# The last stage of an attention and mixture-of-experts kernel: half of each returned row block is added by accumulating transfers

## The chip, the cores and the metric

The kernel runs on one core of one Trainium2 chip. The metric is the device time of one execution in microseconds; lower is better. The time of the kernel before is 515.96 us, the median of three runs (512.97 to 517.47).

## The reference

The input is 64 sequences of 64 tokens, 4096 tokens of 256 numbers. First comes an attention layer over the tokens and a context, then a feed-forward layer of 32 experts, of which each token uses four, with a shared expert beside them:

```python
x = x + attention(layernorm(x), ctx, wq, wk, wv, wo)
h = layernorm(x)
probs = softmax(h @ router.T)
topv, topi = top_k(probs, 4);  topv = topv / sum(topv)
out = sum over the four e of topi: topv[e] * (silu(h @ w_gate[e]) * (h @ w_up[e])) @ w_down[e]
out = out + sigmoid(h @ sgate) * ((silu(h @ sw_gate) * (h @ sw_up)) @ sw_down)
return x + out
```

What matters here is the sum over a token's four experts. Each expert's weighted result is one row of 256 numbers, so a token has four rows to be added to its residual. All of it is in 32-bit floats.

## The kernel before

The 4096 tokens are 32 tiles of 128 (a token of each tile on each partition). The residual of all of them stays in on-chip memory as `resid[p, tile, d]`. The kernel has three stages.

**Attention and routing.** Sixteen blocks of two tiles. GpSimd sends each token's row to its four experts' regions of the tensor `sent` in device memory by indirect transfers.

**Experts.** 68 pairs of row tiles are loaded from `sent`, multiplied with the experts' weights, weighted, and scattered by GpSimd (L512, two transfers for each pair) to the tensor `returned`. A token's four results end side by side there: `returned_v[p, tile, k, d]` (L69), so that the four rows of a token are 4 KB in one piece.

**Last stage.** Half of the shared expert (groups 4 to 7 of `groups` = 8; a group is four tiles) is kept for the end, and the returned rows are added beside it. Its work by engine:

- TensorE, for each group `g` and quarter `f` of the hidden width: the gate product and the up product (`shared_gate_up`, recorded at L806, six matmuls of 512 columns each), then the down product (`shared_down` at L850, `last_down` at L840 for the last group). The up product of quarter `f` waits until VectorE has multiplied quarter `f - 2`, since they share a bank (`shared_act`). The down product waits for the adds of the group before (`shared_added`) and for this group's multiplications.
- ScalarE: the silu of each gate product (L539), and seven stores of a finished group, 512 KB each (`store`, L770). It issues them between the third and the fourth silu of a group, and the rest after the last.
- VectorE, in an order written out by hand: `shared_mul(g, f)` (L1241), and behind it as many `fold`s as `TURNS` gives, one fold for each pair of tiles, 2, 5, 5 and 4 in the four groups. A fold `i` adds rows 2 and 3 onto rows 0 and 1 (L1698), row 1 onto row 0 (L1701), and row 0 onto the residual (L1705). At the end of a group `shared_add(g)` adds the shared expert's result (four instructions, L1269). After the first of these groups comes `split_hn_lo` (L1235).
- SP: once every scatter has landed (`down_sent`, L423), it loads the returned rows of two tiles at a time into one of `YR` = 4 places of the tensor `arena` (`picked`, L426), 16 loads of 1024 KB. Load `i` waits until fold `i - 4` has used its place (`pick_step`). After the last fold it stores the four tiles of the last group, 128 KB each (L431).
- GpSimd: nothing. Its last scatter is issued before SP's first load.

Of the kernel before, what the change touches and what calls it, by code (L numbers as in the profile page):

```python
# [7 lines left out]
ALU = mybir.AluOpType  # L8
# [14 lines left out]
TOP = 4  # L23
# [12 lines left out]
def build_xattn_moe(nc, x, ctx_t, wq_t, wk_t, wv, wo_t, router_t, w_gate_up, w_down,  # L36
# [7 lines left out]
    tiles = tokens // P  # L44
# [11 lines left out]
    SPLIT_FROM = 8  # L56
    HEADS = 4
    DOWNS = 4
    YR = 4
    FIRST_MIXED = 3  # L60
    LEAD = 2 * FIRST_MIXED
    assert blocks >= RING and pairs % 4 == 0 and tokens * TOP == tiles * P * TOP
# [6 lines left out]
    returned_v = returned[P * slot_tiles:P * slot_tiles + tokens * TOP].rearrange("(t p k) d -> p t k d", p=P, k=TOP)  # L69

    with ExitStack() as stack:
        def sb(name, shape, dt=F32):
            return stack.enter_context(nc.sbuf_tensor(name, shape, dt))

        def sem(name):
            return stack.enter_context(nc.semaphore(name))
# [10 lines left out]
        def by_tile(which, n=0):  # L87
            return which[:, n * 2 * D:(n + 1) * 2 * D].rearrange("p (j d) -> p j d", j=2)
# [18 lines left out]
        hn_hi_drain = plain_r[:, 3 * 512:5 * 512].rearrange("p (c t) -> p c t", c=DC)  # L107
        arena = sb("arena", [P, 8192])
        w_dn = arena[0:F, 0:EXPERTS * D].rearrange("f (e d) -> f e d", e=EXPERTS)
        picked = [arena[:, 2048 * n:2048 * n + 2048].rearrange("p (t k d) -> p t k d", t=2, k=TOP)  # L110
                  for n in range(YR)]
        xn, xn_r = by_tile(plain, 0), by_tile(plain_r, 0)
        values = [plain[:, 512 * at:512 * at + 1024].rearrange("p (q d) -> p q d", q=4) for at in (1, 7)]
# [137 lines left out]
        tile_in = [sem(f"tile_in{u}") for u in range(RING)]  # L251
        down_sent = [sem(f"down_sent{u}") for u in range(DOWNS)]
        picked_in = [sem(f"picked_in{u}") for u in range(YR)]

        AMID, BEHIND = groups, EARLY
        POOL_CONSTS = 16
# [6 lines left out]
        def wait(eng, name, count):  # L263
            if count > 0:
                eng.wait_ge(S[name], count)
# [31 lines left out]
        def unit_after(pair):  # L297


            return None  # L300
# [47 lines left out]
        def _(sp):  # L348
# [57 lines left out]
            for pair in range(pairs):  # L406
                u = pair % RING
# [15 lines left out]
                sp.wait_ge(down_sent[u], 32 * (pairs // DOWNS))  # L423
            for i in range(tiles // 2):
                wait(sp, "pick_step", i - YR + 1)
                sp.dma_start(picked[i % YR], returned_v[:, 2 * i:2 * i + 2, :, :]) \  # L426
                    .then_inc(picked_in[i % YR], 16)
            sp.wait_ge(S["pick_step"], tiles // 2)
            for t in range(tiles - GT, tiles):
# [5 lines left out]
        def _(pool):  # L435
# [70 lines left out]
            for pair in range(pairs):  # L506
                u = pair % DOWNS
                wait(pool, "back_ready", pair // 2 + 1)
                wait(pool, "down_ready", pair + 1)
                for s in range(2):  # L510
                    t = 2 * pair + s
                    pool.indirect_dma_start(  # L512
                        out=returned,
                        out_offset=bass.IndirectOffsetOnAxis(ap=back[:, t:t + 1], axis=0),
                        in_=down_e[u][:, s, :], in_offset=None).then_inc(down_sent[u], 16)

        @block.scalar
        def _(act):
# [174 lines left out]
            def experts_to_copy(pair):  # L693

                first = column_of(pair)
                more = 7 if mixed(pair + 2) else 0
                _, values = nc.values_load_multi_w_load_instructions(
                    tile_expert[0:1, first:first + 4 + more], engines=[mybir.EngineType.Activation],
                    min_val=0, max_val=EXPERTS - 1,
                    skip_runtime_bounds_check_because="a tile's first row over the rows of a region "  # L700
                                                      "is the number of an expert")
                copied_e[pair], copied_e[pair + 2] = values[0:4], values[7:11]
# [85 lines left out]
        def _(pe):  # L788
# [288 lines left out]
            def experts_of(pair):  # L1077
                first = column_of(pair) + (4 if mixed(pair) else 0)
                _, values = nc.values_load_multi_w_load_instructions(
                    tile_expert[0:1, first:first + (1 if mixed(pair) else 2)], engines=[mybir.EngineType.PE],  # L1080
                    min_val=0, max_val=EXPERTS - 1,
                    skip_runtime_bounds_check_because="a tile's first row over the rows of a region "
                                                      "is the number of an expert")
                return values
# [105 lines left out]
        def _(dve):  # L1190
# [102 lines left out]
            for n in range(-2, blocks + 5):  # L1293
# [19 lines left out]
                if there(n - 3):  # L1313
                    b = n - 3
                    u = b % RING
# [123 lines left out]
            def made_by(ins, mark=None):  # L1439
                ins.then_inc(S["route_dve"], 1)  # L1440
                made[0] += 1
                if mark is not None:
                    assert MARK[mark] == made[0], (mark, made[0])
                return made[0]

            def after(count):
# [3 lines left out]
            n = made_by(dve.tensor_scalar(count_ci[:, :], count_view, region[:, :], float(QUARTER - 1),  # L1450
                                          ALU.subtract, ALU.add))
# [3 lines left out]
            n = made_by(dve.tensor_scalar(padded_ci[:, 1:2], count_ci[:, :], 5, 5, ALU.logical_shift_right,  # L1455
                                          ALU.logical_shift_left))
# [17 lines left out]
            n = made_by(dve.tensor_tensor(ends_c[:, 1:2], ends_c[:, 1:2], total_view, ALU.add), "ends")  # L1474
            after(n)
            n = made_by(dve.tensor_tensor(starts_c[:, :], ends_c[:, :], padded_c[:, :], ALU.subtract))
            after(n)
            n = made_by(dve.tensor_scalar(shift_c[:, :], starts_c[:, :], region[:, :], None, ALU.subtract))
# [3 lines left out]
            n = made_by(dve.tensor_scalar(mixed_here[:, narrow], tile_no[:, narrow], starts_c[:, 1:2], None,  # L1482
                                          ALU.is_ge))
# [9 lines left out]
            n = made_by(dve.scalar_tensor_tensor(mixed_here[:, narrow], tile_no[:, narrow], ends_c[:, 1:2],  # L1493
                                                 mixed_here[:, narrow], ALU.is_lt, ALU.mult))
# [4 lines left out]
            n = made_by(dve.scalar_tensor_tensor(mixed_new[:, narrow], mixed_at[:, narrow], shift_c[:, 1:2],  # L1499
                                                 tile_no[:, narrow], ALU.add, ALU.subtract))  # L1500
# [6 lines left out]
            n = made_by(dve.scalar_tensor_tensor(mixed_new[:, narrow], mixed_new[:, narrow], float(QUARTER),  # L1507
                                                 mixed_here[:, narrow], ALU.add, ALU.mult))
# [55 lines left out]
            n = made_by(dve.tensor_scalar(gate_den[:, late], gate_den[:, late], 1.0, None, ALU.add))  # L1564
# [76 lines left out]
            def experts_to_copy(pair):  # L1641

                first = column_of(pair)
                more = 7 if mixed(pair + 2) else 0
                _, values = nc.values_load_multi_w_load_instructions(
                    tile_expert[0:1, first:first + 2 + more], engines=[mybir.EngineType.DVE],
                    min_val=0, max_val=EXPERTS - 1,
                    skip_runtime_bounds_check_because="a tile's first row over the rows of a region "
                                                      "is the number of an expert")
                copied_e[pair], copied_e[pair + 2] = values[0:2], values[7:9]  # L1650
# [10 lines left out]
            for pair in range(pairs):  # L1661
# [16 lines left out]
                k = unit_after(pair - 1)  # L1678
                if k is not None and k < 2 * FB and k % 2 == 1:
                    f = k // 2  # L1680
# [12 lines left out]
            def fold(i, g):  # L1693

                wait(dve, "shared_added", GT * g)
                dve.wait_ge(picked_in[i % YR], 16 * (i // YR + 1))
                rows_t = picked[i % YR]
                dve.tensor_tensor(rows_t[:, :, 0:2, :], rows_t[:, :, 0:2, :], rows_t[:, :, 2:4, :], ALU.add) \  # L1698
                    .then_inc(S["fold_step"], 1)
                wait(dve, "fold_step", 2 * i + 1)  # L1700
                dve.tensor_tensor(rows_t[:, :, 0, :], rows_t[:, :, 0, :], rows_t[:, :, 1, :], ALU.add) \  # L1701
                    .then_inc(S["fold_step"], 1)
                wait(dve, "fold_step", 2 * i + 2)
                both = resid[:, 2 * i:2 * i + 2, :]
                dve.tensor_tensor(both, both, rows_t[:, :, 0, :], ALU.add).then_inc(S["pick_step"], 1)  # L1705

            weighed = 0
            for g in range(BEHIND, groups):
                for f in range(FB):
                    shared_mul(g, f)  # L1710
                    while weighed < weighed_by(g, f):
                        fold(weighed, g)
                        weighed += 1
                wait(dve, "pick_step", weighed)
                shared_add(g)
                if g == BEHIND:
                    split_hn_lo(EARLY + 3)
# [45 lines left out]
```

## Time and profile before

| | |
|---|---|
| median of three runs | 515.96 us (512.97 to 517.47) |
| span of the profiled execution | 667.5 us; no other time of that execution is given |
| TensorE busy | 574.4 us (86%) |
| VectorE busy | 363.5 us (54%) |
| ScalarE busy | 288.7 us (43%) |
| GpSimd busy | 269.4 us (40%) |
| last stage, first load of returned rows to last add | 602.73 to 665.35 us |

The profile is of one execution, whose span is 151.5 us longer than the median of the runs. Times in the trace count from its start. An engine's busy time is the time in which an instruction of it was in work; a row of a timeline gives the start, the length, the engine, the line of the kernel, the operation and its operands, and in brackets how long the engine had been idle before it and what ended that. Matmuls overlap in the records, so that the start of one and the start of the next tell more than the length. "DMA share" is the mean busy share of the sixteen DMA engines; it can be a little over 1.

### The profile page before, as it was taken

How to read it: one execution, taken by the hardware profiler on the slowest of the kernel's cores; microseconds unless marked ns; L12 is line 12 of the kernel's file. 1: busy time of each engine (PE TensorE's matmuls, PEld its weight loads, DVE VectorE, ACT ScalarE, POOL GpSimd, SP SyncE). 2: the span in 40 equal slices, each digit the busy share in tenths (PEclk: the TensorE clock that was granted, in tenths of full speed). 3: DMA queues.
4: the chain of work that ended last, by engine and by line, in shares of the span. 5: the costliest groups of instructions: out<-in, count | busy, mean ns of one | idle time of the engine just before them, and what ended most of it. 6: DMA issues, size and time to landing. Idle time of an engine off the chain costs nothing. (4 is left out here: it accounts for less than half of the span.)

```text
span 667.5 us, 13365 instructions
## 1 busy us (share of the span) xinstructions
PE 574.4 (86%) x3945; PEld 478.3 (72%) x3945; DVE 363.5 (54%) x1199; ACT 288.7 (43%) x719; POOL 269.4 (40%) x344
## 2 busy tenths in 40 slices
PE   8998787788887777899998988778877898979998
PEld 7997777677777565677886666656666676658886
DVE  5575455555555351565553635445454444536998
ACT  5775444555444440613463545444454544401111
POOL 1004444445555458380034544445454454560000
PEclk9999788987778788699997977988989978989999
DMA  5573544444433322293145444544444544228996
GB/s 160 181 227 128 170 156 129 144 134 145 138 123 113 110 76 107 70 244 98 31 130 148 131 140 124 140 136 139 130 140 140 150 131 132 87 86 330 368 340 230
DMA packets 65956, 100.77 MB, mean 151 GB/s; under 512 B 9856, under 2 KB 52864, under 8 KB 65792
## 3 DMA queue, kind: packets, MB, share of 16 engines
q1 hardware_dynamic: 48704, 60.30, 30.6%
q0 software_dynamic: 12672, 35.41, 14.7%
q10 hardware_dynamic: 4512, 4.23, 1.9%
q8 instruction: 34, 0.56, 0.4%
q14 instruction: 34, 0.28, 0.1%
HBM read 55.92 MB, written 43.97 MB: 150 GB/s over the span
## 5 line engine op out<-in xcount | busy, mean ns | idle before, releaser
L512 POOL DMA_INDIRECT returned<-arena,back x136 | 130.6, 960 | 171.7 <-DVE back L1629 81.5
L481 POOL DMA_INDIRECT sent<-rows,slot x128 | 129.9, 1015 | 159.2 <-issue 82.7
L1100 PE MATMUL bank<-w_gu,arena 128*128 x416 | 94.7, 363 | 26.6 <-issue 16.6
L1100 PEld LDWEIGHTS bank<-w_gu,arena 128*128 128x128 f32 x416 | 73.0, 205 | 32.8 <-issue 32.8
L1580 DVE TENSOR_TENSOR arena<-bank,arena 128x192 f32<-128x192 f32 x68 | 24.2, 356 | 113.5 <-ACT arena L737 94.5
L737 ACT ACTIVATE arena<-bank 128x192 f32<-128x192 f32 x68 | 22.3, 329 | 127.0 <-remote 70.5
L806 PE MATMUL bank<-w_hi_all,att_split 128*128 128x256 f32 x256 | 56.8, 314 | 18.6 <-issue 18.6
L1597 DVE TENSOR_SCALAR arena<-bank,back_to 128x256 f32<-128x256 f32 x136 | 59.0, 476 | 6.3 <-remote 5.3
L806 PE MATMUL bank<-att_split,w_hi_all 128*128 128x256 f32 x256 | 55.5, 336 | 1.4 <-issue 1.3
L710 ACT COPY hnt<-w_gu 128x384 f32 x128 | 55.7, 509 | 0.0
L806 PEld LDWEIGHTS bank<-w_hi_all,att_split 128*128 128x128 f32 x256 | 42.4, 208 | 18.2 <-issue 18.2
L806 PE MATMUL bank<-hnt_rounded,ws_hi 128*128 128x512 f32 x160 | 51.0, 412 | 2.6 <-issue 2.6
L806 PEld LDWEIGHTS bank<-att_split,w_hi_all 128*128 128x128 f32 x256 | 47.7, 248 | 4.7 <-issue 4.6
L539 ACT ACTIVATE act_t<-bank 128x512 f32<-128x512 f32 x24 | 14.2, 598 | 82.9 <-PE bank L806 66.6
L1049 PE MATMUL bank<-ident_r,loaded 128*128 128x128 f32 x272 | 46.0, 295 | 0.4 <-issue 0.4
L850 PE MATMUL bank<-ws_d,act_t 128*128 128x256 f32 x192 | 43.3, 381 | 1.0 <-DVE act_t L1241 1.0
L731 ACT COPY arena<-bank 128x512 f32<-128x512 f32 x68 | 39.5, 582 | 8.9 <-PE bank L1049 2.5
L850 PEld LDWEIGHTS bank<-ws_d,act_t 128*128 128x128 f32 x192 | 36.1, 190 | 6.4 <-DVE act_t L1241 1.4
L806 PEld LDWEIGHTS bank<-hnt_rounded,ws_hi 128*128 128x128 f32 x160 | 31.6, 197 | 10.9 <-issue 4.0
L1049 PEld LDWEIGHTS bank<-ident_r,loaded 128*128 128x128 f32 x272 | 32.6, 148 | 9.0 <-issue 2.8
L806 PE MATMUL bank<-w_lo_all,att_split 128*128 128x256 f32 x128 | 30.3, 310 | 6.8 <-issue 6.5
L1311 DVE TENSOR_REDUCE negmax<-bank 128x2 f32<-128x256 f32 x16 | 6.7, 422 | 51.8 <-remote 51.8
(216 smaller groups left out, 1128.6 us busy)
## 6 DMA issues: line engine op xcount, KB each, us to landing
arena<-returned SPq DMA_DIRECT2D x16, 1024.0 KB, 7.2
loaded<-sent SPq DMA_DIRECT2D x104, 134.0 KB
w_gu<-w_gate_up SPq DMA_DIRECT2D x32, 192.0 KB
sent<-rows SPq DMA_DIRECT2D x4, 1072.0 KB, 6.2
loaded<-sent SPq DMA_DIRECT2D x128, 33.5 KB
resid<-x SPq DMA_DIRECT2D x16, 256.0 KB, 2.9
att_plain<-ctx_t SPq DMA_DIRECT2D x16, 256.0 KB, 3.1
out<-resid ACTq DMA_DIRECT2D x7, 512.0 KB, 4.9
```

What stands on the lines that cost most here:

```text
L481: pool.indirect_dma_start(out=sent, out_offset=bass.IndirectOffsetOnAxis(ap=slot[:, 2 * b + j, k:k + 1], axis=0), in_=rows[:, u, j, :], in ...
L512: pool.indirect_dma_start(out=returned, out_offset=bass.IndirectOffsetOnAxis(ap=back[:, t:t + 1], axis=0), in_=down_e[u][:, s, :], in_offs ...
L539: act.activation(act_t[:, f, :], gate_banks[f % 2][:, :], ACT.Silu) \
L710: last = act.copy(gu_copy[:, q, :, :], w_gu[:, :, bass.ds(copied_e[pair][q], 1), :] .rearrange("p c e f -> p c (e f)"))
L731: act.copy(gt[pair % 2].rearrange("p s c q -> p (s c q)"), gt_banks[pair % 2][:, :]) \
L737: act.activation(act_e[pair % 2], gu_views[pair % 2][:, :, 0:F], ACT.Silu) \
L806: last = pe.matmul(out_view, stationary(s_part, c), moving(m_part, c), start=(n == 0 and c == 0), stop=(n == 2 and c == DC - 1))
L850: last = pe.matmul(sum_banks[t // 2][:, 256 * (t % 2):256 * (t % 2) + 256], act_t[:, f, P * t:P * t + P], ws_d[:, f, :], start=(f == 0 and ...
L1049: last = pe.transpose(gt_banks[pair % 2][:, at:at + P].bitcast(F32R), loaded[:, u, s, P * c:P * c + P], ident_r[:, :])
L1100: last = pe.matmul(view[:, s, :], rows_t[:, s, c, :], w_gu[:, c, bass.ds(e[s - 2 + len(e)], 1), :] .rearrange("p e f -> p (e f)"), start=( ...
L1580: dve.tensor_tensor(act_e[pair % 2], gu_views[pair % 2][:, :, F:2 * F], act_e[pair % 2], ALU.mult).then_inc(S["act_e_ready"], 1)
L1597: last = dve.tensor_scalar(down_e[u][:, s, :], down_banks[pair % 2][:, D * s:D * s + D], back_to[:, pair // 2 % 4, 2 * (pair % 2) + s, 0:1 ...
```

## The change

The number of places for returned rows goes from four to eight, each of half the size: a place now holds two rows of each token instead of four. SP's load `i` brings rows 0 and 1 of each token of two tiles (512 KB, 2 KB in one piece for a token). GpSimd waits for that load to land and issues a transfer of rows 2 and 3 that adds them onto what lies in the place (`accum_op=ALU.add`, 512 KB), with a semaphore of its own for each place. VectorE waits for that, and its fold has two instructions instead of three: row 1 onto row 0, and row 0 onto the residual. SP's load `i` waits for fold `i - 8`.

```diff
-    YR = 4
+    YR = 8
...
-        picked = [arena[:, 2048 * n:2048 * n + 2048].rearrange("p (t k d) -> p t k d", t=2, k=TOP)
+        picked = [arena[:, 1024 * n:1024 * n + 1024].rearrange("p (t k d) -> p t k d", t=2, k=2)
                   for n in range(YR)]
...
+        folded_in = [sem(f"folded_in{u}") for u in range(YR)]
...
             for i in range(tiles // 2):
                 wait(sp, "pick_step", i - YR + 1)
-                sp.dma_start(picked[i % YR], returned_v[:, 2 * i:2 * i + 2, :, :]) \
+                sp.dma_start(picked[i % YR], returned_v[:, 2 * i:2 * i + 2, 0:2, :]) \
                     .then_inc(picked_in[i % YR], 16)
...
+            for i in range(tiles // 2):
+                pool.wait_ge(picked_in[i % YR], 16 * (i // YR + 1))
+                pool.dma_start(picked[i % YR], returned_v[:, 2 * i:2 * i + 2, 2:4, :], accum_op=ALU.add) \
+                    .then_inc(folded_in[i % YR], 16)
...
             def fold(i, g):
 
                 wait(dve, "shared_added", GT * g)
-                dve.wait_ge(picked_in[i % YR], 16 * (i // YR + 1))
+                dve.wait_ge(folded_in[i % YR], 16 * (i // YR + 1))
                 rows_t = picked[i % YR]
-                dve.tensor_tensor(rows_t[:, :, 0:2, :], rows_t[:, :, 0:2, :], rows_t[:, :, 2:4, :], ALU.add) \
-                    .then_inc(S["fold_step"], 1)
-                wait(dve, "fold_step", 2 * i + 1)
                 dve.tensor_tensor(rows_t[:, :, 0, :], rows_t[:, :, 0, :], rows_t[:, :, 1, :], ALU.add) \
                     .then_inc(S["fold_step"], 1)
-                wait(dve, "fold_step", 2 * i + 2)
+                wait(dve, "fold_step", i + 1)
                 both = resid[:, 2 * i:2 * i + 2, :]
                 dve.tensor_tensor(both, both, rows_t[:, :, 0, :], ALU.add).then_inc(S["pick_step"], 1)
```

## Rows read from the trace of the kernel before

**Rows 1.** The head of the page: span, and busy time of two engines.

```profile
span 667.5 us, 13365 instructions
PE 574.4 (86%) x3945; PEld 478.3 (72%) x3945; DVE 363.5 (54%) x1199; ACT 288.7 (43%) x719; POOL 269.4 (40%) x344
```

**Rows 2.** The chain that ended last, in order: start us, us, what.

```profile
593.17 0.13 issue
...
611.13 10.90 PE bank L806 x48
622.03 6.91 PE bank L850 x32
...
646.99 10.93 PE bank L806 x48
657.92 6.92 PE bank L840 x32
...
664.87 0.48 DVE resid L1269
```

**Rows 3.** Busy time by stretch: us, each engine, granted clock, DMA share, GB/s.

```profile
602.73:665.35 62.62, 62.10 (x279) 52.24 (x277) 56.33 (x78) 8.84 (x14) 0.00 (x0) 1.00 0.89 331
...
613.03:648.22 35.19, 35.19 (x159) 29.61 (x158) 34.44 (x48) 4.36 (x8) 0.00 (x0) 1.00 0.96 356
```

**Rows 4.** VectorE's timeline, 607 to 665 us.

```profile
607.73 1.23 DVE L1698 TENSOR_TENSOR arena<-arena 128x1024 f32<-128x1024 f32 x1 [2.71 <-DMA arena<-returned]
...
613.03 1.66 DVE L1269 SCALAR_TENSOR_TENSOR resid<-bank,shared_gate,resid 128x256 f32<-128x256 f32 x4
614.60 1.22 DVE L1235 TENSOR_TENSOR hnt_rounded<-hnt,hnt_rounded 128x1024 fp32r<-128x1024 f32 x1
615.74 0.68 DVE L1241 TENSOR_TENSOR act_t<-bank,act_t 128x512 f32<-128x512 f32 x1
...
631.18 1.66 DVE L1269 SCALAR_TENSOR_TENSOR resid<-bank,shared_gate,resid 128x256 f32<-128x256 f32 x4
...
662.73 0.89 DVE L1269 SCALAR_TENSOR_TENSOR resid<-bank,shared_gate,resid 128x256 f32<-128x256 f32 x2
664.01 0.48 DVE L1269 SCALAR_TENSOR_TENSOR resid<-bank,shared_gate,resid 128x256 f32<-128x256 f32 x1 [0.38 <-PE bank L840]
```

**Rows 5.** VectorE's groups from 602 us: line, operands, count | busy, mean ns.

```profile
L1698 DVE TENSOR_TENSOR arena<-arena 128x1024 f32<-128x1024 f32 x16 | 19.5, 1217 | 2.7 <-DMA arena<-returned 2.7
L1701 DVE TENSOR_TENSOR arena<-arena 128x512 f32<-128x512 f32 x16 | 11.1, 693 | 0.5
L1705 DVE TENSOR_TENSOR resid<-resid,arena 128x512 f32<-128x512 f32 x16 | 11.1, 692 | 0.5
```

**Rows 6.** TensorE's timeline, group 5, third gate and third up product.

```profile
616.42 0.61 PE L806 MATMUL bank<-hn_hi,ws_hi 128*128 128x512 f32 x2
...
617.78 0.61 PE L806 MATMUL bank<-hn_hi,ws_hi 128*128 128x512 f32 x2
```

**Rows 7.** SP's loads of returned rows: its timeline, their landing, its waits.

```profile
602.73 45.84 SPq L426 DMA_DIRECT2D arena<-returned  x16
...
DMA to landing us min/median/max: 4.9/7.2/11.1
...
SPq L426 <- DVE resid L1705: 39.2, 12, 5.6
```

**Rows 8.** DMA queues, 602 us to the end (q1 is SP's, q10 ScalarE's).

```profile
q1 hardware_dynamic: 4928, 17.30, 69.2%
q10 hardware_dynamic: 3696, 3.67, 16.4%
```

**Rows 9.** Busy time by stretch of four us, as in rows 3.

```profile
646.00:650.00 4.00, 4.00 (x19) 3.35 (x18) 3.90 (x8) 0.60 (x1) 0.00 (x0) 1.00 1.03 416
```

**Rows 10.** GpSimd's timeline, its last two scatters of 128 rows.

```profile
598.97 0.96 POOL L512 DMA_INDIRECT returned<-arena,back  x1 [0.30 <-issue]
600.24 0.96 POOL L512 DMA_INDIRECT returned<-arena,back  x1 [0.30 <-issue]
```

## The prediction

> **What bounds the kernel now.** I read four views of the last stage, the only one that the change touches. First the chain of waits [rows 2]: from 593.17 us to 664.87 it is TensorE's matmuls and nothing else, group after group (gate and up products 10.90 us, down product 6.91 us, so 17.8 us a group); only the last add, 0.48 us, is VectorE's. Second the busy times [rows 3]: TensorE is busy 62.10 of 62.62 us at a granted clock of 1.00 (its upper level, 2.4 GHz). 48 matmuls of 512 columns in 10.90 us are 227 ns each; 512 columns at 2.4 GHz are 213 ns, so there is hardly a gap to win. VectorE is busy 56.33 us, and between the adds of group 4 and group 6 34.44 of 35.19 us: nearly full, yet not the bound, as the chain doesn't pass through it. Third, its timeline [rows 4]: it begins a group's adds 1.9 us behind TensorE (613.03 against 611.13 [rows 2]), but nobody waits for them, as the next down product comes 9 us later (622.03). At the very end it waits for TensorE again, 0.38 us. Fourth the transfers [rows 3, 7, 8]: the DMA engines have a busy share of 0.89 over the whole stretch, 0.96 in its middle. They are the least noticed and second fullest resource here.
>
> **The time it is counted against.** All durations are of one execution with a span of 667.5 us [rows 1], whose time without the profiler isn't given; the median of the runs is 515.96 us, 151.5 us less. TensorE's last stage runs at 227 ns for 213 ns of columns, so it can't be much shorter in a run without the profiler, and the missing 151.5 us must lie in the stages before. So I work out microseconds in the last stage and add them to 515.96.
>
> **What goes.** Sixteen instructions at L1698, 1.22 us each, 19.5 us of VectorE [rows 5]. They lie beside TensorE. TensorE's chain doesn't shorten: gain 0. What VectorE finishes earlier at the end, the first two adds (0.89 us at 662.73 [rows 4]), still has the fourth add behind TensorE's last matmul. One wait and increment of VectorE in each fold go too, hidden the same way.
>
> **What comes, and stays hidden.** SP issues 16 loads as before, half the bytes each. It waited 39.2 us for places [rows 7]; with eight places it runs further ahead, which costs nothing by itself. Eight more semaphores: 0, outside the chain. ScalarE's stores are unchanged. GpSimd was idle in this stage; its 16 issues stand behind its last scatter (600.24 [rows 10]) and wait for SP's loads, and nothing is queued behind them. The issue: the trace has no direct transfer of GpSimd's. The nearest is the scatter of 128 rows, which repeats every 1.27 us (600.24 - 598.97 [rows 10]). The new one names 256 pieces of 2 KB; between 1.27 us and three times that (two times the pieces, two reads for one write), 3.8 us. I take 2.5 us, under the pace of the transfers below.
>
> **What comes, and doesn't stay hidden: the DMA engines.** From 602 us to the end (65.5 us) SP's queue took 69.2% of the engines' time, 45.3 us, and ScalarE's 16.4%, 10.7 us [rows 8]. The seven stores of 512 KB cost 10.7 / 7 = 1.53 us each. SP's four small stores are one more such, so its 16 loads cost 43.8 us, 2.74 us each, and 1.37 us for half of one. An accumulating transfer of 512 KB isn't in the trace. Below: it costs as a plain one of its bytes, 1.37 us. Above: it reads the 512 KB that lie in the place besides the 512 KB from device memory, so it takes the engines as long as a 1024 KB load, 2.74 us. I take the upper one: the old contents have to come through the engine as well. The sum until the last fold has its data, with six stores (9.2 us) among it:
>
> - before: 16 x 2.74 + 9.2 = 53.0 us of the 62.6 us that TensorE gives;
> - after, lower end: 16 x (1.37 + 1.37) + 9.2 = 53.0 us, as before;
> - after, upper end: 16 x (1.37 + 2.74) + 9.2 = 75.0 us.
>
> The Trainium skill ("Collectives: The Full Stack", section "The bandwidth ceiling: the fold count and why AG ≠ RS ≠ AR") says that a reducing transfer emits two read descriptors for one write on the same ring and so runs at half a copy's rate, measured 1.93. By it an addition would cost 1.93 x 1.37 = 2.64 us (an estimate), and the sum would be 16 x (1.37 + 2.64) + 9.2 = 73.4 us; by the rows alone it is anything from 53.0 to 75.0. No row of this case shows an accumulating transfer.
>
> Full engines show a share of 1.03 [rows 9], so 75.0 us of work take 72.8 us. The first load landed at 607.73 [rows 4]; at 416 GB/s [rows 9] its 1.05 MB took 2.5 us, so the clock for the work, landing delay included, starts at 605.2. The last accumulating transfer lands at 605.2 + 72.8 = 678.0. Behind it on VectorE come the last fold, 2 x 0.69 us [rows 5], and four adds, 1.66 us [rows 4]: 681.0, where the last add ended at 665.35 before (664.87 + 0.48). That is +15.7 us. With all loads at the best rate (2.52 us for 1024 KB) it is 60.5 + 9.2 = 69.7 us, hence 677.9 and +12.6 us. I take +15 us: 531 us.
>
> **The new wait at the start.** Half a load lands at about 605.2 + 1.3 = 606.5; GpSimd then issues, and if it takes as long from issue to first byte as SP did (602.73 to 605.2), the first addition starts at 609.0. It shares the engines with SP's other loads, so it takes double: 2.5 us at the lower price, 5.0 at the upper. The first fold's data is there at 611.5 or 614.0 instead of 607.7, the second's at 614.0 or 619.0. Behind the two folds VectorE has the adds, the split and the first product of group 5: 1.4 + 1.6 + 1.1 + 0.7 us [rows 4, 5], ready at 618.8 or 623.8. Who waits for that is TensorE's third up product, due at 617.78 [rows 6]: a stall of 1.0 or 6.0 us. At the upper price it isn't added, as the DMA engines' sum already ends later.
>
> **The rivals.**
>
> 1. *An accumulating transfer costs as a plain one.* For it: the place is on chip, and reading it may lie beside the read from device memory. Then the engines have 53.0 us of work as before, TensorE stays the bound, and only the start's stall is left: +1.0 us, 517 us, no change. This is the other side; it decides at the point where 16 x (1.37 + c) + 9.2 passes the 62.6 us less the later start, about c = 2.0 us. Chance 0.24.
> 2. *The issue or the small pieces bind.* If GpSimd needs 3.8 us an issue, the last goes out at 606.5 + 61 = 667.5 and lands some 5 us later: 672.5, +10 us with the work behind it, 526 us. If every added piece costs three plain ones, the engines have 16 x 5.48 + 9.2 = 96.9 us: +37 us, 553 us. Chance 0.12 together, half for each.
> 3. *VectorE was a bound that the profiled execution hides.* For it: 34.44 of 35.19 us busy. Against: no wait of TensorE for it. If TensorE did wait in other runs for adds that come late by 1.9 and 2.2 us (631.18 [rows 4] against 622.03 + 6.91 [rows 2]) and the like, up to 6 us go: 510 us. Chance 0.08.
>
> **How the numbers follow.** The forecast has 0.56. A change of 1% (5.2 us) is about what a measurement of this kernel can tell from none. Slower by more: forecast and rival 2, 0.68. Within: rival 1, 0.24. Faster by more: 0.08. The forecast's own range is 526 to 536 (a cost of 2.5 to 2.9 us for an addition, and TensorE's stalls placed otherwise). The range for 8 in 10 takes in rival 1 with the spread of the runs below it, hence from 515, and to 542 for an addition that costs somewhat over two loads; left out are rival 3 and the dear half of rival 2.
>
> **What would show it.** In the changed profile: the DMA share near 1.0 from 606 us until the last addition; issue to landing of GpSimd's transfers 5 us or more, and the last landing near 678 us; VectorE idle before the first of a fold's two instructions, waiting for `arena<-returned`; TensorE waiting for VectorE's `act_t` or `resid` at L806 and L850, and its chain broken. L1698 gone, the fold 1.4 us instead of 2.6. I am wrong if the added transfers take the engines 1.4 us each, if the chain is still TensorE's alone, or if GpSimd's issues follow each other at their own length with the DMA share well under 1.

## The result: 2.7% slower

The changed kernel takes 529.61 us, the median of four runs (526.37 to 531.96), against 516.45 us of the kernel before on the same chip. The ratio is 1.0269 (95% interval 1.0216 to 1.0321); the medians differ by 13.2 us, and the ratio makes it 13.9. The forecast was 531, from 515 to 542.

The profile after is of an execution with a span of 524.1 us. That of before had 667.5 us [rows 1]. The two spans can't be set against each other; the last stages can, as the first experiment shows. From the page after come the span, the busy times and the chain's shares by engine:

```profile
span 524.1 us, 13365 instructions
...
PE 503.7 (96%) x3945; PEld 430.7 (82%) x3945; DVE 346.3 (66%) x1183; ACT 285.4 (54%) x719; POOL 290.2 (55%) x360
...
DMA 10%; PE 4%; POOL 1%; DVE 1%; issue 1%; DVEq 0%; SPq 0%; POOLq 0%
```

The chain was TensorE's alone [rows 2]; now transfers in it take 10% of the span. The chain in order, start us, us, what:

```profile
444.79 4.08 DMA arena<-returned
448.87 0.59 issue
449.46 1.31 POOL arena L520
450.76 12.63 DMA arena<-returned
...
464.93 9.48 DMA arena<-returned
474.41 0.34 issue
474.76 23.01 DMA arena<-returned
...
509.37 4.41 PE bank L812 x18
513.78 6.92 PE bank L846 x32
```

The transfers set the pace until 497.8 us. At the very end two paths meet: VectorE's last four adds begin at 519.38, and TensorE's last down product ends at 520.70 and releases the last of them.

The next rows are the busy time of the last stage, first load to last add, and of a stretch near its start in which TensorE first stands still (until 468.39) and then runs at its lower clock (columns as in [rows 3]):

```profile
444.79:521.21 76.42, 64.28 (x273) 52.60 (x272) 37.72 (x62) 8.23 (x13) 19.29 (x16) 0.93 1.07 269
461.00:473.00 12.00, 4.61 (x11) 3.65 (x12) 8.18 (x15) 0.00 (x0) 3.58 (x3) 0.59 1.10 265
```

The stage was 62.62 us with a DMA share of 0.89 [rows 3]; it is 76.42 us with 1.07. The DMA engines are busier and yet move less: 269 GB/s instead of 331. VectorE's and GpSimd's groups of the stage (columns as in [rows 5]):

```profile
L1708 DVE TENSOR_TENSOR resid<-resid,arena 128x512 f32<-128x512 f32 x16 | 11.1, 692 | 0.5
L1704 DVE TENSOR_TENSOR arena<-arena 128x512 f32<-128x512 f32 x16 | 11.1, 691 | 37.6 <-DMA arena<-returned 37.6
L520 POOL DMA_DIRECT2D arena<-returned x16 | 19.3, 1212 | 40.1 <-DMA arena<-returned 39.9
```

Who waited for whom from 455 us on (total us, times, longest us):

```profile
POOL arena L520 <- DMA arena<-returned: 33.7, 11, 4.2
PE bank L812 <- DVE act_t L1247: 10.3, 2, 9.7
```

The DMA queues from 446 us to the end (q0 is GpSimd's), and the additions with their median us from issue to landing:

```profile
q0 software_dynamic: 4352, 8.39, 58.2%
q1 hardware_dynamic: 4922, 8.90, 33.7%
q10 hardware_dynamic: 3696, 3.67, 14.4%
...
arena<-returned POOLq DMA_DIRECT2D x16, 512.0 KB, 21.1
```

L1698's 19.5 us [rows 5] are gone, and VectorE now waits 37.6 us for `arena<-returned`, where it waited 2.7. GpSimd's sixteen issues are 1.2 us each and it waited 40.1 us in all, so it isn't the bound. Its queue (q0) and SP's (q1) moved nearly the same bytes in the stretch, 8.39 and 8.90 MB, and the additions took 58.2% of the engines' time against 33.7%; SP's share has the four last stores in it (1.5 us, taken from the forecast). Over 78 us that is 45.4 us for 16 additions, 2.84 us each, and (26.3 - 1.5) / 16 = 1.55 us for a plain load of 512 KB. The forecast had 2.74 and 1.37.

### The profile page after: what moved, and what is told of

It reads as the page before. It is cut to its first block and busy times, and to the rows that moved or that the text cites. A ratio compares the mean times of both kernels' runs of the same rounds, so it can differ in the third digit from the quotient of the medians.

```text
span 524.1 us, 13365 instructions
## 1 busy us (share of the span) xinstructions
PE 503.7 (96%) x3945; PEld 430.7 (82%) x3945; DVE 346.3 (66%) x1183; ACT 285.4 (54%) x719; POOL 290.2 (55%) x360
## 5 line engine op out<-in xcount | busy, mean ns | idle before, releaser
L1106 PE MATMUL bank<-w_gu,arena 128*128 x416 | 83.7, 338 | 0.7 <-DVE resid L1275 0.3
L1106 PEld LDWEIGHTS bank<-w_gu,arena 128*128 128x128 f32 x416 | 65.8, 190 | 1.6 <-issue 1.4
L812 PE MATMUL bank<-w_hi_all,att_split 128*128 128x256 f32 x256 | 48.7, 292 | 0.0
L812 PE MATMUL bank<-att_split,w_hi_all 128*128 128x256 f32 x256 | 44.0, 284 | 0.2 <-DVE att_split L1306 0.2
L1055 PE MATMUL bank<-ident_r,loaded 128*128 128x128 f32 x272 | 42.9, 282 | 0.3 <-DMA loaded<-sent 0.3
L520 POOL DMA_DIRECT2D arena<-returned x16 | 19.3, 1212 | 40.1 <-DMA arena<-returned 39.9
L812 PEld LDWEIGHTS bank<-w_hi_all,att_split 128*128 128x128 f32 x256 | 37.2, 191 | 0.9 <-issue 0.9
L812 PEld LDWEIGHTS bank<-att_split,w_hi_all 128*128 128x128 f32 x256 | 36.5, 192 | 0.6 <-DVE att_split L1306 0.4
L1055 PEld LDWEIGHTS bank<-ident_r,loaded 128*128 128x128 f32 x272 | 30.5, 141 | 7.6 <-DMA loaded<-sent 1.3
L1704 DVE TENSOR_TENSOR arena<-arena 128x512 f32<-128x512 f32 x16 | 11.1, 691 | 37.6 <-DMA arena<-returned 37.6
## 6 DMA issues: line engine op xcount, KB each, us to landing
arena<-returned POOLq DMA_DIRECT2D x16, 512.0 KB, 21.1
```

The costliest lines, as they stand in the source:

```text
L520: pool.dma_start(picked[i % YR], returned_v[:, 2 * i:2 * i + 2, 2:4, :], accum_op=ALU.add) \
L812: last = pe.matmul(out_view, stationary(s_part, c), moving(m_part, c), start=(n == 0 and c == 0), stop=(n == 2 and c == DC - 1))
L1055: last = pe.transpose(gt_banks[pair % 2][:, at:at + P].bitcast(F32R), loaded[:, u, s, P * c:P * c + P], ident_r[:, :])
L1106: last = pe.matmul(view[:, s, :], rows_t[:, s, c, :], w_gu[:, c, bass.ds(e[s - 2 + len(e)], 1), :] .rearrange("p e f -> p (e f)"), start=( ...
```

## The experiments

All ratios are to the kernel before, run on the same chip; "stage" is the time from the first load of returned rows to the end of the last add, from the trace. The four kernels whose names end in 2 ran on a chip on which the kernel before takes 656.3 us (median of seven). The others ran on two chips on which it takes 515.18 us (`changed_again`, `four_places`, `first_two`, `all_but_two`) and 514.81 us (`again_before3`, `no_accum3`, `no_first_add3`, `eight_but_two`).

| kernel | time us | ratio (95%) | more us | stage us |
|---|---|---|---|---|
| before (`again_before2`) | 656.17 | one run | | 62.6 |
| before (`again_before3`) | 515.85 | one run | | 61.8 |
| changed (`changed_again`) | 531.22 | 1.0323 (1.0263 to 1.0383) | 16.6 | 76.8 |
| `no_accum2` | 655.80 | 1.0008 (0.9918 to 1.0097) | 0.5 | 68.1 |
| `no_accum3` | 517.97 | 1.0104 (1.0062 to 1.0145) | 5.4 | 68.3 |
| `more_plain2` | 667.90 | 1.0190 (1.0105 to 1.0276) | 12.5 | 75.4 |
| `no_first_add2` | 652.16 | 0.9858 (0.9757 to 0.9959) | -9.3 | 63.5 |
| `no_first_add3` | 512.46 | 0.9958 (0.9918 to 0.9998) | -2.2 | 61.3 |
| `first_two` | 524.39 | 1.0167 (1.0102 to 1.0231) | 8.6 | 71.4 |
| `eight_but_two` | 526.75 | 1.0240 (1.0186 to 1.0295) | 12.4 | 73.6 |
| `four_places` | 537.64 | 1.0457 (1.0376 to 1.0537) | 23.5 | 81.9 |
| `all_but_two` | 535.85 | 1.0392 (1.0318 to 1.0466) | 20.2 | 83.0 |

("More us" is the ratio less one, times the median of before on that chip. By the same rule the changed kernel's first result is 13.9.)

**The kernel before again**, to have a base for the stage.

> The kernel before, unchanged, for a trace whose span is near the median of its runs (the trace of before had 667.5 us against 516). Engine-time theory: the last stage, first load of returned rows to last add, is 62 to 63 us as in the first trace, and TensorE is busy without a gap in it. If the profiled stage was distorted, it differs by more than 2 us, and the sum of the prediction stood on a wrong base.

> The kernel before, unchanged, once more for a trace: if it lands near 516 us, its last stage can be set beside those of the changed kernel at the same pace of the stages before. Expected: 62.6 us from the first load of returned rows to the last add, TensorE without a gap, as in both traces so far, whose spans were 654 and 668 us.

The second landed near 516 us. VectorE's timeline in it, the first fold and the last add:

```profile
454.40 1.23 DVE L1698 TENSOR_TENSOR arena<-arena 128x1024 f32<-128x1024 f32 x1 [3.92 <-DMA arena<-returned]
...
510.83 0.48 DVE L1269 SCALAR_TENSOR_TENSOR resid<-bank,shared_gate,resid 128x256 f32<-128x256 f32 x1 [0.26 <-PE bank L840]
```

Its span is 513.5 us. From the first load at 449.46 to 511.31 are 61.8 us; it is 62.6 us in the traces with spans of 654 and 668 us. So the sum in microseconds of the stage could be carried over, and what differs between the chips lies in the stages before it. The mean granted clock of the whole execution is 0.92 in `again_before2` and 1.00 in `again_before3`; why, and whether that is all of the difference, was not studied.

**The addition itself: `no_accum`.** One word of the changed kernel goes.

```diff
-                pool.dma_start(picked[i % YR], returned_v[:, 2 * i:2 * i + 2, 2:4, :], accum_op=ALU.add) \
+                pool.dma_start(picked[i % YR], returned_v[:, 2 * i:2 * i + 2, 2:4, :]) \
```

> The changed kernel with GpSimd's sixteen transfers as plain ones: they write over the place instead of adding, so rows 0 and 1 of each token are left out of the sum. All waits, issues, sizes and the 2 KB pieces stay. Theory (an addition costs the DMA engines two plain transfers): 53 us of work instead of 75, time 517 to 518 us, about 12 us under the changed kernel. Rival (the chain SP load, wait, GpSimd issue, or the small pieces bind): 526 to 530 us, as the changed kernel.

> The changed kernel with GpSimd's transfers as plain ones (rows 0 and 1 of each token are overwritten, so left out of the sum), again, since the first measurement was uncertain by 1% and its trace showed TensorE standing still once, behind the first two folds, with a last stage of 68 us against 62.6. Engine-time theory alone: +1 us. With the late start as a cost of its own, which the chain load, wait, issue, second transfer has even with plain transfers: +5 to +6 us. Rival (GpSimd's issue or the small pieces make the whole loss): +13 to +16 us.

The first measurement couldn't tell 0 from 5 us. The second gives +5.4 us (1.0104, by the interval 3.2 to 7.5), where the changed kernel has +13.9 and +16.6. So some two thirds of the loss come from adding in a transfer, with the same bytes and waits.

The expectation said that the 2 KB pieces stay too, and that was not so. The page after and the page of `no_accum3` have the same bytes in GpSimd's queue, in 2048 packets fewer (packets, MB, share):

```profile
q0 software_dynamic: 17024, 43.80, 27.3%
q0 software_dynamic: 14976, 43.80, 23.1%
```

Without the addition each of the sixteen transfers went out as 128 pieces of 4 KB, with it as 256 of 2 KB, and GpSimd's issue took 0.71 instead of 1.20 us in the median. The issues are hidden behind GpSimd's waits in both. The smaller pieces alone are an unlikely cause: SP's plain loads in 2 KB pieces cost 1.55 us for 512 KB in the changed kernel, not 2.84. A plain transfer in 2 KB pieces from GpSimd was not run.

About a third of the loss stays without any addition. The second trace shows where, in VectorE's timeline:

```profile
457.58 0.69 DVE L1704 TENSOR_TENSOR arena<-arena 128x512 f32<-128x512 f32 x1 [10.73 <-DMA arena<-returned]
```

and among the waits of its last stage:

```profile
PE bank L812 <- DVE act_t L1247: 4.7, 1, 4.7
```

The first fold's data comes 11.8 us after the first load (457.58 - 445.82); with one load of all four rows it is 4.9 us (454.40 - 449.46). TensorE stands still once for it, 4.7 us, and never again. Below, this is called the late start: the first fold waits for a load, an issue and a second transfer in a row.

**Engine time without additions: `more_plain`.** The kernel before, with a plain load of 512 KB more for each fold.

```diff
+        spare_in = [sem(f"spare_in{u}") for u in range(12)]
+        spare = w_gu.rearrange("p c e f -> p (c e f)")
...
                     .then_inc(picked_in[i % YR], 16)
+                if i >= 12:
+                    sp.wait_ge(spare_in[i % 12], 16)
+                sp.dma_start(spare[:, 1024 * (i % 12):1024 * (i % 12) + 1024]
+                             .rearrange("p (t k d) -> p t k d", t=2, k=2),
+                             returned_v[:, 2 * i:2 * i + 2, 2:4, :]).then_inc(spare_in[i % 12], 16)
```

> The kernel before, with its four places, three-instruction folds and no work for GpSimd, and behind each of SP's 16 loads another plain load of 512 KB into memory that is free in this stage (nothing reads it). Theory (engine time alone makes the loss): 16 x (2.74 + 1.37) + 9.2 = 75 us of work for the DMA engines, as in the changed kernel, less 1.4 us since nothing waits for the last one: +10 to +14 us, 526 to 530 us. Rival (it is the latency of an addition or of the chain through GpSimd): no change, 516 to 518 us.

+12.5 us (7 to 18 by the interval), and a stage of 75.4 us where the changed kernel has 76.4 and 76.8. (The trace is of the longest of its four runs, 677.05 us.) There is no work for GpSimd and no addition, and the first fold's data comes 5.1 us after the first load (601.88 - 596.82), so there is no late start either: DMA work alone makes a loss of this size. VectorE waited nine times for its data, 2.0 us at most, where in [rows 4] it waited once:

```profile
DVE arena L1707 <- DMA arena<-returned: 14.7, 9, 2.0
```

TensorE's longest standstill in the stage is then 2.4 us:

```profile
PE bank L849 <- DVE act_t L1250: 2.4, 1, 2.4
```

**VectorE's relief: `no_first_add`.** The kernel before without L1698.

```diff
-                dve.tensor_tensor(rows_t[:, :, 0:2, :], rows_t[:, :, 0:2, :], rows_t[:, :, 2:4, :], ALU.add) \
-                    .then_inc(S["fold_step"], 1)
-                wait(dve, "fold_step", 2 * i + 1)
```

> The kernel before without the first of a fold's three instructions (rows 2 and 3 of each token are loaded but left out of the sum): VectorE has 19.5 us less to do, transfers as before. Theory (TensorE is the bound, VectorE's relief is worth nothing): 516 us, within 0.3%. Rival (VectorE was a hidden bound): up to 6 us less, 510 us.

> The kernel before without the first of a fold's three instructions (rows 2 and 3 of each token are left out of the sum), again, since the first measurement gave 0.986 with an interval of 0.976 to 0.996 where 1.00 was expected, while its trace had the same last stage. Theory (VectorE's relief is worth nothing): within 0.5% of the kernel before. Rival (VectorE is a bound in part of the runs): 0.98 to 0.99 again.

The ratio is 0.9858 in the first and 0.9958 in the second, with more runs and a narrower interval. The first one's runs spread from 644.80 to 666.85 us, and its trace has a stage of 63.5 us, no shorter than before. The trace of the second has a stage 0.5 us shorter than `again_before3`'s, and VectorE waiting for TensorE in groups 5, 6 and 7, as in its timeline here:

```profile
493.32 1.66 DVE L1269 SCALAR_TENSOR_TENSOR resid<-bank,shared_gate,resid 128x256 f32<-128x256 f32 x4 [3.56 <-PE bank L850]
```

So 19.5 us of VectorE's work are most likely worth 2.2 us, 0.1 to 4.2 by the interval, and of these the trace shows 0.5. The first figure, which spoke for rival 3, did not come back at its size; that a small part of it is real stays possible.

**Late start or full engines: four placements.** The changed kernel's trace has both at once. TensorE's timeline at the start of the stage shows the standstill, and behind it matmuls at half the pace, 0.85 us from pair to pair instead of 0.45. The granted clock is 0.90 from 460 to 464 us, 0.50 (1.2 GHz) from 464 to 472, 0.65 from 472 to 474, and 1.00 behind that:

```profile
458.12 0.62 PE L812 MATMUL bank<-hnt_rounded,ws_hi 128*128 128x512 f32 x2
468.39 1.22 PE L812 MATMUL bank<-hn_hi,ws_hi 128*128 128x512 f32 x2 [9.66 <-DVE act_t L1247]
469.41 1.05 PE L812 MATMUL bank<-hn_hi,ws_rounded 128*128 128x512 f32 x2
...
474.02 0.62 PE L812 MATMUL bank<-hn_hi,ws_rounded 128*128 128x512 f32 x2
```

The next kernels choose which folds get an addition. The first three have the four places of the kernel before:

```diff
+        def added(i):
+            return True        # four_places;  i < 2: first_two;  i >= 2: all_but_two
...
+                n = 2 if added(i) else TOP
+                sp.dma_start(picked[i % YR][:, :, 0:n, :], returned_v[:, 2 * i:2 * i + 2, 0:n, :]) \
...
+            for i in filter(added, range(tiles // 2)):
+                pool.wait_ge(picked_in[i % YR], 16 * (i // YR + 1))
+                pool.dma_start(picked[i % YR][:, :, 0:2, :], returned_v[:, 2 * i:2 * i + 2, 2:4, :],
+                               accum_op=ALU.add).then_inc(folded_in[i % YR], 16)
```

> The changed kernel once more, as the measure for its neighbours on the same chip: 13 us over the kernel before. In its first trace two things happen at once: the DMA engines are full from 448 us to the last addition (4.2 us a fold and its share of the stores), and TensorE stands still for 9.7 us at the first addition and then runs some products at its lower clock. Either would explain the 13 us; the next three kernels tell them apart.

> The changed kernel with four places instead of eight, so that SP has at most four plain loads ahead of the first additions. Engine-time theory (75 us of work have to be done by the last fold): no change against the changed kernel, +13 us over the kernel before. Late-start theory (the loss is made by the first two additions, which share the engines with eight plain loads): the first addition lands some 3 us earlier, and the loss falls to +8 to +10 us.

> The kernel before with its four places, but the first two folds (i = 0, 1) get their rows 2 and 3 by GpSimd's additions, the other fourteen as before. DMA work 53.0 + 2 x 1.37 = 55.7 us. Engine-time theory: it fits under TensorE's 62.6 us, and only the later start is paid, 0 to +3 us. Late-start theory: the whole standstill at the first two additions is there, 7 to 10 us, and about 2 us at the lower clock behind it: +8 to +12 us.

> The kernel before with its four places, folds 0 and 1 as before, the other fourteen with additions. DMA work 53.0 + 14 x 1.37 = 72.2 us. Engine-time theory: the last fold's data lands only 2.7 us earlier than with sixteen additions: +10 to +11 us. Late-start theory: TensorE doesn't stand still at the start, and the loss is 0 to +3 us.

`first_two` has +8.6 us with two additions only, where the engine-time theory said 0 to +3: the late start has this price by itself. Its waits have one standstill of TensorE:

```profile
PE bank L819 <- DVE act_t L1254: 7.1, 1, 7.1
```

and its chain in order, from 471 us on, is TensorE alone again:

```profile
485.40 11.16 PE bank L819 x48
496.56 6.91 PE bank L863 x32
503.46 10.93 PE bank L819 x48
514.39 6.92 PE bank L853 x32
```

`four_places` and `all_but_two` came out dearer than either theory said, +23.5 and +20.2 us. Their traces point to a third limit, the round of a place: the time from a place's load to the end of the fold that frees it. In `four_places` the median us to landing of SP's loads and of GpSimd's additions:

```profile
arena<-returned SPq DMA_DIRECT2D x16, 512.0 KB, 7.3
arena<-returned POOLq DMA_DIRECT2D x16, 512.0 KB, 9.3
```

and GpSimd's wait for the loads:

```profile
POOL arena L527 <- DMA arena<-returned: 53.2, 13, 11.6
```

A place passes through the load (7.3 us), the addition (9.3, GpSimd's issue of 1.2 within it) and the fold (1.4): 18 us, and four places give a fold every 4.5 us. Measured are (528.44 - 460.84) / 15 = 4.5 us from fold to fold, with eight places (517.93 - 459.73) / 15 = 3.9. TensorE needs 3.6 (a group of 17.8 us has five folds).

That the two 4.5 agree proves little: a round divided by the places in use gives the pace whatever the limit is, and with eight places it is (9.5 + 21.1 + 1.4) / 8 = 4.0. What speaks for the places is the comparison with the changed kernel, from which `four_places` differs in their number (and in the gap that half-filled places leave between the tokens' rows). The DMA engines' share in the stage falls from 1.07 to 1.01, what they move from 269 to 251 GB/s, and the time rises by 7 us. So the eight places are a needed part of the change. For the question asked, two of the three kernels were spoiled by their lack. The fourth has plain 1024 KB loads for folds 0 and 1 and then eight places:

```diff
+        def place(i):
+            n = 2 * i if i < 2 else (4 + i - 2) % 8
+            k = 2 if added(i) else TOP
+            return arena[:, 1024 * n:1024 * n + 512 * k].rearrange("p (t k d) -> p t k d", t=2, k=k)
+
+        def free_after(i):
+            return {6: 1, 7: 1, 8: 2, 9: 2}.get(i, i - 7 if i > 9 else 0)
```

> Folds 0 and 1 with plain 1024 KB loads as in the kernel before, the other fourteen with additions, and places as in the changed kernel: the first two loads take half of the memory, four half-size places the other half, and from fold 2 on there are eight half-size places. DMA work 72.2 us. The four-place kernel with fourteen additions had a round of a place (fold, load, issue, addition) for a limit as well; here that is gone. Engine-time theory: the last addition lands 2.7 us earlier than in the changed kernel: +11 to +13 us over the kernel before. Late-start theory (the standstill at the first two additions makes the loss): 0 to +4 us. A result of +5 to +9 us would say that each has a part.

+12.4 us, within what the engine-time theory said (+11 to +13). The first two folds are on time, the first addition of all is late, and the last fold's data still comes at 519.75, 70.1 us after the first load:

```profile
454.66 1.22 DVE L1720 TENSOR_TENSOR arena<-arena 128x1024 f32<-128x1024 f32 x1 [3.95 <-DMA arena<-returned]
...
469.43 0.69 DVE L1723 TENSOR_TENSOR arena<-arena 128x512 f32<-128x512 f32 x1 [6.07 <-DMA arena<-returned]
...
519.75 0.69 DVE L1723 TENSOR_TENSOR arena<-arena 128x512 f32<-128x512 f32 x1 [1.43 <-DMA arena<-returned]
```

This kernel isn't free of a late start, though: it only moved it to fold 2. TensorE stands still there for 5.1 us and has a granted clock of 0.50 from 472 to 476 us; its waits in the stage (total us, times, longest us):

```profile
PE bank L825 <- DVE act_t L1260: 6.2, 3, 5.1
```

The kernel with the engines' work alone is `more_plain2`, with +12.5 us. So the late start alone costs 8.6 us and the engines' work alone about 12.5, and together they cost 14 to 17, not 21. The intervals of the single times are too wide to show this by themselves, but the stages say the same: 9.6 us longer (`first_two`) and 12.8 (`more_plain2`) alone, 14.6 and 15.0 together. The two overlap, as the DMA engines work on while TensorE stands still (their share is 1.10 from 461 to 473 us), and that time is not lost twice.

## Why the prediction was right

**The bound before.** TensorE, as the chain said: `no_first_add3` gains 0.4% for 19.5 us less of VectorE. "Gain 0" was right to 2 us or so. Rival 3's 6 us are outside the interval.

**The carry-over of microseconds** from a trace of 667.5 us to runs of 516 us was right: the stage took 62.6 and 61.8 us.

**The price of an addition.** This was the choice that decided. The prediction took the upper end, 2.74 us; 2.84 were measured. The lower end, 1.37, was rival 1's. `no_accum3` moves the same bytes without the addition, at 1.36 us for one of GpSimd's transfers (32.1% of 68 us for sixteen), and loses 5.4 us instead of 14 to 17. The rule quoted from the Trainium skill ("Collectives: The Full Stack", section "The bandwidth ceiling: the fold count and why AG ≠ RS ≠ AR"), two reads for one write and half a copy's rate, agrees with these runs: an addition's 2.84 us are 1.8 times SP's 1.55 and 2.1 times GpSimd's plain 1.36. The page states it for a reduction between cores, and the traces here show the price, not the two reads.

**The sum.** The forecast for the last fold's data was 75.3 us after the first load is issued (678.0 - 602.73). Measured: 517.93 - 444.79 = 73.1. For the stage it was 78.3 us (681.0 - 602.73), measured 76.4 and 76.8. The engines' work was a little larger, 45.4 + 24.8 + six stores of 1.6 = 79.8 us instead of 75.0, and their share while full was 1.10 instead of 1.03. The two deviations nearly cancel, which is luck; the agreement to 2 us is better than the terms. The path at the end was right only by a hair: TensorE, which lost time of its own at the start, finished with the transfers and not before them, and the four adds behind the last fold took 1.82 us instead of 1.66.

**GpSimd's issue.** 2.5 us were taken, 1.2 us measured, hardly more than a scatter of 128 rows. It wasn't in the sum. Rival 2 was wrong in both halves: no issue of 3.8 us, and no piece at the price of three plain ones.

**The signs** that the prediction named are there: DMA share 1.10, 21.1 us from an addition's issue to its landing, VectorE waiting for `arena<-returned`, TensorE for `act_t`, the chain broken, L1698 gone.

**The late start** was the term that was mis-sized. The prediction had a stall of 1.0 us at the plain price and 6.0 at the upper. Measured are 4.7 (`no_accum3`) and 9.66 us. The lower clock behind it, which the prediction didn't have at all, costs some 2.5 us more (468.39 to 473.56 for twelve matmuls that take 2.7 us at 227 ns). The first fold's data was forecast at 11.3 us after the first load (614.0 - 602.73) and came at 14.9 (459.73 - 444.79). At the upper price this changed little, as it was said to be covered by the engines' sum, and it nearly was: 12.5 us without it (`more_plain2`), 14 to 17 with it. But rival 1's time would have been too low: at a plain transfer's price the kernel would have been 1% slower (`no_accum3`, +5.4 us) and not 1.0 us, at the edge of what the prediction counted as a change.

**What wasn't foreseen** is the round of a place. The prediction said that eight places cost nothing, which stands; it didn't see that four would have cost 7 us more.

## What to carry to other kernels

An accumulating transfer moved work from VectorE to the DMA engines here at the price of about two loads of its bytes, so first look at their busy share in that stage: at 0.89 there was no room for half as much again, however idle GpSimd was. A load and a transfer that waits for it have two landings in a row, so the first result comes later and a place is held longer: the number of places must be at least the round of a place divided by the wanted time from one result to the next. An experiment that takes out one flag can change more than that flag: look at the packets, as in `no_accum3`. And work taken from an engine that the chain doesn't pass through was worth next to nothing (2.2 of 19.5 us), even at 98% busy.

## What the runs showed of the hardware

A 2 KB piece of an accumulating transfer took the DMA engine 176 ns in the median; in SP's queue a plain piece of 2 KB took 84 to 98 ns and one of 4 KB 159 ns. GpSimd's plain transfers in `no_accum3` went out in 4 KB pieces, about 170 ns each, the changed kernel's accumulating ones of the same shape in 2 KB pieces. TensorE's granted clock fell to the lower level in the standstill of 9.66 us (0.50 from 464 us on) and came back some 5 us after it worked again; from 480 to 500 us it is 1.00. The times of single pieces are medians over the transfer records of the last stage.
